# Normalising all chunks at the beginning of two causal stages, four score banks for their first maxima, and a reordered start of linear attention

## The reference

```python
x = x + sublayer_i(layernorm(x))        # i = 0 .. 7
```

```python
# 2 and 4, for each chunk of 512 tokens
scores = einsum('bhqd,bhkd->bhqk', q, k) * 8 ** -0.5
attn = softmax(where(causal, scores, -inf))      # in 4: -10000 for -inf
x = x + (einsum('bhqk,bhkd->bhqd', attn, v)) @ w_o + b_o
# 0: S_t = diag(exp(g_t)) S_{t-1} + k_t v_t^T ; o_t = q_t^T S_t, then a gate and a product
# 5: h = silu(x @ w1 * s1) * (x @ w2 * s2), two more layers, x @ w3 * s3
```

## Time and profile before

| what | value |
|---|---|
| three runs | 1694.02, 1687.55, 1692.11 us; median 1692.11 us |
| profiled execution | 1689.31 us, span 1687.6 us |
| TensorE's clock over the span | 0.883 of the full clock granted |
| busy share of the span | TensorE 83%, VectorE 62%, GpSimd 45%, ScalarE 44% |
| stage 0 | begins with VectorE at 8.44 us |
| stage 2 | from 321.7 us |
| stage 4 | from 642.4 us |

### The profile page before, as it was taken

How to read it: one execution, slowest core, us unless ns; L and a number is a source line. 1 busy time by engine, 2 the same in 40 slices (tenths; PEclk the granted TensorE clock), 3 DMA queues, 4 the chain that set the end, 5 groups by cost and what they waited for, 6 DMA issues and landing times. The chain is left out here.

```text
span 1687.6 us, 24930 instructions
## 1 busy us (share of the span) xinstructions
PE 1395.5 (83%) x8907; PEld 849.4 (50%) x8907; DVE 1042.6 (62%) x2864; ACT 747.3 (44%) x1169; POOL 763.4 (45%) x833
## 2 busy tenths in 40 slices
PE   5576688789998795999977999899999999985193
PEld 3354566644454562444435777555554545534062
DVE  5766678567884646688833222578778777757112
ACT  4554244336665341566644333455455454430041
POOL 5442344423432555354443442356555455563533
PEclk9688789859999796699978999799999999997597
DMA  3000004200000322000001020000000000003213
GB/s 97 7 8 1 34 22 193 85 1 1 1 2 1 129 63 97 1 2 1 2 0 53 1 100 1 1 1 1 1 1 1 1 1 1 1 1 125 63 51 100
DMA packets 29562, 52.74 MB, mean 31 GB/s; under 512 B 3216, under 2 KB 24592, under 8 KB 27264
## 3 DMA queue, kind: packets, MB, share of 16 engines
q1 hardware_dynamic: 26144, 44.36, 7.5%
q0 software_dynamic: 3296, 6.78, 1.2%
HBM read 29.07 MB, written 21.02 MB: 30 GB/s over the span
## 5 line engine op out<-in xcount | busy, mean ns | idle before, releaser
L2502 DVE CUSTOM_DVE_ANT_0 s_masked_scores<-s_for_max,s_mask_qk 128x128 bf16<-128x128 f32 (+3 forms) x512 | 227.0, 486 | 58.3 <-PE s_for_max L2323 56.4
L2863 POOL TENSOR_TENSOR wbuf<-s_probs 128x1024 f32<-128x1024 f32 x64 | 152.0, 2374 | 201.9 <-ACT s_probs L3022 201.9
L3022 ACT ACTIVATE s_probs<-s_scores 128x1024 f32<-128x1024 f32 x128 | 132.2, 1033 | 202.2 <-PE s_scores L2944 202.2
L2270 POOL TENSOR_SCALAR_AFFINE_SELECT s_probs<-s_probs 128x256 f32<-128x256 f32 x256 | 99.9, 407 | 247.7 <-ACT s_probs L2429 149.6
L3064 DVE TENSOR_REDUCE s_negmax<-s_for_max 128x2 f32<-128x1024 f32 x126 | 152.2, 1208 | 21.4 <-PE s_for_max L2919 21.3
L2323 PE MATMUL s_for_max<-s_k_stack,s_q_stack 32*128 32x128 f32 (+3 forms) x512 | 142.6, 441 | 26.9 <-DVE s_max_wide L2502 17.5
L3071 DVE RECIPROCAL s_recip<-s_pv_and_sums 128x128 f32<-128x128 f32 x128 | 116.6, 934 | 47.3 <-PE s_pv_and_sums L2970 47.3
L2323 PEld LDWEIGHTS s_for_max<-s_k_stack,s_q_stack 32*128 32x128 f32 x512 | 72.3, 205 | 128.8 <-DVE s_max_wide L2502 87.0
L2429 ACT ACTIVATE s_probs<-s_scores 128x1024 f32<-128x1024 f32 x128 | 127.4, 1024 | 14.0 <-PE s_scores L2344 13.7
L2957 PE MATMUL s_pv_and_sums<-s_probs,s_v 128*64 128x512 f32 x512 | 123.9, 605 | 0.9 <-DVE wbuf L3079 0.9
L2358 PE MATMUL s_pv<-s_probs,s_v_and_one 128*32 128x512 f32 (+3 forms) x1024 | 96.9, 474 | 1.5 <-DVE s_o L2521 1.5
(11 more groups left out here) (574 smaller groups left out, 3431.3 us busy)
## 6 DMA issues: line engine op xcount, KB each, us to landing
rows_by_expert<-s_empty_rows SPq DMA_DIRECT2D x8, 1032.0 KB, 10.5
s_w<-extra SPq DMA_DIRECT2D x2, 2048.0 KB, 10.1
wbuf<-w SPq DMA_DIRECT2D x1, 3460.0 KB, 11.2
s_generators<-extra SPq DMA_DIRECT2D x1, 2898.0 KB, 12.8
wbuf<-w SPq DMA_DIRECT2D x1, 2888.0 KB, 9.7
wbuf<-w SPq DMA_DIRECT2D x1, 2124.0 KB, 8.1
dispatched<-s_empty_slots SPq DMA_DIRECT2D x1, 2064.0 KB, 8.5
s_rows<-dispatched SPq DMA_DIRECT2D x8, 258.0 KB, 2.8
```

The costliest lines, as they stand in the source:

```text
L2270: last = nc.gpsimd.affine_select(out=diag, in_=diag, compare_op=ALU.is_ge, fill=0.0, base=0, pattern=[[0, diag.shape[1]], [1, P]], channel ...
L2502: last = nc.vector.tensor_tensor_reduce(out=junk[:, m % 2, at:at + n], in0=p1[m % 2][:, at:at + n], in1=mask[:, S - n:S], scale=1.0, scala ...
L2863: nc.gpsimd.tensor_tensor(added[half], probs[:, g % 2, 2 * half, :, :], probs[:, g % 2, 2 * half + 1, :, :], ALU.add).then_inc(s_added, 1)
L3022: nc.scalar.activation(probs[:, g % 2, j, :, :], p2[:, :, :], ACT.Exp, scale=dh ** -0.5).then_inc(s_exp, 1)
```

## The change

1. Start: each of the four transfers of x has a semaphore of its own; SyncE no longer waits for them, and VectorE waits for a chunk before its statistics.
2. Stage 0: TensorE makes 10, 2, 2 and 5 idle products (`spare_products`, of the bf16 identity into an unused bank) at the start and between its first steps, and waits for the weights only ahead of the first projection; the values of chunk 0 stand behind the sums of the log decay on TensorE, its gates behind factors 0 and 1 on ScalarE, and its copies behind the first scaled keys on VectorE.
3. Stages 2 and 4: the rows of all chunks are normalised, by VectorE, turned and copied in the beginning, into idle halves of p2, no longer through `pm`. The first 20 units of maxima take four banks in turn (p1 and p2[1]'s halves). The first exponentials wait for the turned rows and these units. GpSimd makes the low parts and adds the bias ahead of the first cut (stage 2: all chunks; stage 4: hs and bias of two chunks, the other two in single steps between cuts).
4. Stage 5: the rstd of chunk 1 stands behind one low part of the weights instead of five.
5. Stage 6: `ones` is cleared ahead of the rstd.

```diff
+    def spare_products(self, bank, n):
+        for _ in range(n):
+            self.nc.tensor.matmul(bank, self.identb[:, :],
+                                  self.identb[:, :].unsqueeze(1).broadcast_to([P, TPC, P]), start=True, stop=True)
...
# stage 0, TensorE
-            pe.wait_ge(sh.wsem[stage], 16)
+            unused = ps_a[:, heads - 1, :]
+            sh.spare_products(unused, 10)
+            pe.wait_ge(ln.s_rstd, 1)
+            sh.spare_products(unused, 2)
...
             ln.turned(pe, 0)
+            sh.spare_products(unused, 2)
+            pe.wait_ge(sh.wsem[stage], 16)
             project(0)
             ln.turned(pe, 1)
-            values(0)
+            sh.spare_products(unused, 5)
             pe.wait_ge(s_const, 5)
             sums(0)
             same(0)
+            values(0)
             project(1)
...
# stage 0, ScalarE
-            gates(0)
             sums(0)
             factors_all(0)
             factors(0, range(2))
+            gates(0)
             project(1)
             factors(0, range(2, 4))
...
# stage 0, VectorE
             log_decay(0)
-            values(0)
             for c in range(2, B):
                 ln.scaled(dve, c)
             near_first(0)
             scaled(0, range(2))
+            values(0)
             gate_input(1)
...
# stage 5, GpSimd
-            split.gpsimd(pool, range(1, 2 + n))
+            split.gpsimd(pool, range(1, 2))
+            ln.rstd_of(pool, 1)
+            split.gpsimd(pool, range(2, 2 + n))
...
# stages 2 and 4, the plan
-    for c in range(1, B):
-        behind(("max", QUADS * c - 2, 3), ("ln", c))
+    plan.insert(plan.index(("q", 0)), ("rows", 1))
+    behind(("q", 0), ("ln", 1))
+    behind(("q_stack", 0), ("rows", 2), ("rows", 3))
+    behind(("k", 0), ("ln", 2))
+    behind(("max", 0, 1), ("ln", 3))
...
+    turned_in = [None, p2[0][:, 0:S], p2[0][:, S:2 * S], p2[0][:, 0:S]]
+    ring = [p1[0], p1[1], p2[1][:, 0:S], p2[1][:, S:2 * S]]
...
+    def unit_bank(m):
+        return ring[m % 4] if m < EARLY_UNITS else p1[m % 2]
...
+    def bank_last_read(m):
+        if m < EARLY_UNITS:
+            return m - 3
+        return m - 3 if m < EARLY_UNITS + 2 else m - 1
...
# GpSimd
-        ln.rstd_of(pool, 0)
+        for c in range(2):
+            ln.rstd_of(pool, c)
+        pool.wait_ge(ln.s_xn, TPC)
         nc.gpsimd.memset(mask[:, :], 0.0).then_inc(s_mask, 1)
...
-        ln.rstd_of(pool, 1)
+        for c in range(2, B):
+            ln.rstd_of(pool, c)
+        pool.wait_ge(s_stack, 2)
...
-        ln.scaled_by(nc.gpsimd, pool, 1)
-        add_bias(0)
-        for c in range(2, B):
-            ln.rstd_of(pool, c)
+        for c in range(1, B):
+            ln.low_part_by(nc.gpsimd, pool, c)
+        if s_hs is None:
+            for c in range(B):
+                add_bias(c)
+        else:
+            for c in range(2):
+                for step in range(1 + TPC):
+                    make_hs(pool, c, step)
+                add_bias(c)
...
-            c = q // QUADS + 1
-            if c < B and q % QUADS == 0:
-                ln.low_part_by(nc.gpsimd, pool, c)
-            if c + 1 < B and q % QUADS == 1:
-                ln.scaled_by(nc.gpsimd, pool, c + 1)
-            if c < B and q % QUADS == 2:
-                add_bias(c)
+                c, step = divmod(q - 1, 2 + TPC)
+                if s_hs is not None and r == 0 and 0 <= c < B - 2:
+                    if step <= TPC:
+                        make_hs(pool, c + 2, step)
+                    else:
+                        add_bias(c + 2)
...
# TensorE
+            elif n == 0:
+                pe.wait_ge(ln.ready, B)
+            else:
+                pe.wait_ge(s_neg, EARLY_UNITS)
...
             elif item[0] == "ln":
-                odd_bank(item)
-                ln.turned(pe, item[1], pm)
+                if item[1] == 3:
+                    pe.wait_ge(ln.ready, 2)
+                ln.turned(pe, item[1], turned_in[item[1]])
...
# VectorE
+        ln.stats_of(dve, 1)
         ln.scaled(dve, 0)
         dve.wait_ge(sh.wsem[stage], 16)
         set_bias()
         st.end()
+        ln.stats_of(dve, 2)
         before_vector(dve)
-        ln.stats_of(dve, 1)
         ln.low_part(dve, 0)
-        for c in range(2, B):
-            ln.stats_of(dve, c)
-        dve.wait_ge(s_mask, 2)
-        dve.wait_ge(s_wide, 1)
+        ln.stats_of(dve, 3)
...
+            if item[0] == "rows":
+                ln.scaled(dve, item[1])
...
+                if m == 0:
+                    dve.wait_ge(s_mask, 2)
+                    dve.wait_ge(s_wide, 1)
```

More of the change, by code:

```diff
@@ L1978, in _ @@
                     nc.gpsimd.tensor_copy(empty[:, :, D], empty_i[:, :]).then_inc(s_empty, 1)
-                if c + 1 < B:
+                if c and c + 1 < B:
                     ln.rstd_of(pool, c + 1)
@@ L2214, in causal_attention @@
     plan = causal_plan()
-    odd = [item for item in plan if item[0] in ("q", "k", "maxT", "v", "oT", "y", "ln")]
+    odd = [item for item in plan if item[0] in ("q", "k", "maxT", "v", "oT", "y")]
+    turned_in = [None, p2[0][:, 0:S], p2[0][:, S:2 * S], p2[0][:, 0:S]]
[6 more added lines that the diff above has]
+        return m - 3 if m < EARLY_UNITS + 2 else m - 1
     block = ctx.enter_context(nc.Block())
@@ L2222, in emptied @@
             return s_stack, 2 * n + "qk".index(what) + 1
-        return {"maxT": s_sub, "v": s_v32, "oT": s_oTs, "y": s_x, "ln": ln.ready}[what], n + 1
+        return {"maxT": s_sub, "v": s_v32, "oT": s_oTs, "y": s_x}[what], n + 1
     @block.sync
@@ L2318, in scores_for_max @@
                 pe.wait_ge(s_stack, 2 * q + 2)
-            if m >= 2:
-                pe.wait_ge(s_neg, m - 1)
+            if bank_last_read(m) > 0:
+                pe.wait_ge(s_neg, bank_last_read(m))
             for x, i, at in max_units(u):
                 rows, n = slice(32 * x, 32 * x + 32), (i + 1) * P
-                last = nc.tensor.matmul(p1[m % 2][:, at:at + n], stacks[0][rows, q % SLOTS, i * P:n],
+                last = nc.tensor.matmul(unit_bank(m)[:, at:at + n], stacks[0][rows, q % SLOTS, i * P:n],
                                         stacks[1][rows, q % SLOTS, 0:n], start=True, stop=True)
@@ L2420, in _ @@
             elif item[0] == "ln":
-                ln.copied(act, item[1], pm[:, :])
+                ln.copied(act, item[1], turned_in[item[1]])
             elif item[0] == "exp_done":
@@ L2611, in first_rows_scalar, with make_hs @@
             ln.copied(act, 0)
[L2613 removed]
+        def make_hs(pool, c, step):
             ts = slice(c * TPC, (c + 1) * TPC)
[L2615 to L2620 removed]
+            if step == 0:
+                pool.wait_ge(ln.s_mv, (c + 1) * TPC)
+                nc.gpsimd.tensor_scalar(rstd[:, ts], ln.mv[:, ts, 1], LN_EPS, 1.0, ALU.add, ALU.mult).then_inc(s_once, 1)
+                pool.wait_ge(s_once, 2 * c + 1)
+                nc.gpsimd.tensor_tensor(rstd[:, ts], rstd[:, ts], sh.mhalf[:, ts], ALU.pow).then_inc(s_once, 1)
+            else:
+                t = c * TPC + step - 1
+                pool.wait_ge(s_once, 2 * c + 2)
                 nc.gpsimd.tensor_scalar(sh.hs[:, t, :], sh.x[:, t, :], ln.mv[:, t, 0:1], rstd[:, t:t + 1],
                                         ALU.subtract, ALU.mult).then_inc(s_hs, 1)
[L2623 removed]
         ca, cab = gen["ca_w"], gen["ca_b"]
```

44 lines of the change are left out of this document (18 added, 26 removed).

## The result

The kernel after takes 1668.3 us (median of four runs, 1662.25 to 1669.23) against 1691.5 before: ratio 0.9866, 95% interval 0.9843 to 0.9890, faster by more than half a per cent. On another chip, in the same series as the last experiments, the ratio was 0.9886 (0.9860 to 0.9912). The prediction was 1663.1, in a range of 1648 to 1676.

| stage | before | after | difference | predicted |
|---|---|---|---|---|
| start and stage 0, to stage 1's begin | 197.37 | 197.47 | +0.1 | -1.3 |
| 2 | 227.80 | 220.23 | -7.6 | -9.7 |
| 4, attention | 226.11 | 215.98 | -10.1 | -9.2 |
| 5 | 156.08 | 152.51 | -3.6 | -6.0 |
| all others | 880.2 | 879.8 | -0.4 | 0 |

What follows compares the result with a forecast made beforehand. One chain of eight stages on one core; in the causal beginnings no engine is saturated, two score banks making TensorE and VectorE wait in turn. 1.3 + 9.7 + 9.2 + 6.0 = 26.2 us off 1689.3 gives 1663.1, range 1648 to 1676.

Steps and rivals of the forecast that it cites:

- Stage 0: Start and stage 0: earlier x shrinks against one added table load and possible standstill; -1.3 us, bounds gain 5, loss 1.
- Stages 2 and 4, banks: Beginnings of stages 2 and 4: four banks remove VectorE's waits for maxima, 2.6 to 5.2 us; -4.0 each.
- near 0: Sign: VectorE's waits for maxima in the first 20 units would be near 0.
- The shift: Stage 2's begin: statistics of chunks 1 and 2 moved into waits; -0.9 us (0 to -1.05); in stage 4 -0.4.
- The first change of chunk: Stages 2 and 4: TensorE's 0.74 and VectorE's 3.17 us standstills as bounds; -1.8 us each stage.
- The second and third: Later chunk changes in stages 2 and 4, at full clock: 12.49 to 11.00 us, 1.49 each; -3.0 a stage.
- rival C: Stages 2 and 4: without turned rows at the chunk change the clock rises late; slower, 1690 and more; chance 0.05.
- GpSimd in stage 4: Ahead of stage 4's first cut: 6.1 us of work added to 14.15 idle, cut 4.4 earlier; 3 to 4 slack left.
- Stage 5: Early rstd brings scaling before h is needed: gap goes, 3.0 us; clock stays up, another 3.0; -6.0 (-3 to -6.5).
- A: Rival: denser beginnings raise the clock early, about 6 us a stage; 1657 for one stage, 1651 both; chance 0.27.
- B: Rival: the beginning gives little, TensorE held by projections and transposes, stage 5's clock falls; about 1675; 0.18 with D.
- D: Rival: banks do nothing, the exponentials' wait on 20 units replacing removed waits; 1671; counted with B, together 0.18.

Runs made afterwards that it cites:

- old order: Kernel after with chunk 0's values and gates back in their old places in stage 0, single waits and idle products kept; 1663.2 us in one run.
- two banks: Kernel after with the first 20 units of maxima on two banks in turn and first exponentials not waiting for them; 1678.9 us, in another series.
- kernel before with idle products: Kernel before plus only idle products in the causal stages' beginnings and quads 0 to 3; first reciprocals 67.8 and 63.2 us, stage 5 152.7.
- after twice: Two profiles of the kernel after, the second unchanged on the combined kernels' chip; stage 5 152.5 and 152.4 us.
- idle products: Kernel after plus idle products in TensorE's waits of both causal stages' beginnings; stage 2 215.0 us, stage 4 215.7.
- x at once: Kernel with stage 0's old order and idle products, SyncE again waiting for all of x before stage 0; stage 1 begins at 194.3 us.
- filled changes: Kernel after with one score product of the fourth unit made five times in quads 2, 6 and 10; stage 2 218.8 us, stage 4 220.2.
- idle in quads: Kernel after plus idle products in causal stages' beginnings and three ahead of each q and k projection of quads 1 to 3; stages 210.3 and 210.5 us.
- no idle: Kernel with stage 0's old order, without the nineteen idle products and their wait; stage 1 begins at 197.1 us.
- scaling first: Kernel after with stage 5's chunk 1 normalised on VectorE before the first h, GpSimd waiting for it; stage 5 151.3 us.
- combined kernel: Kernel after with stage 0's old order, stage 5's scaling first and idle products in beginnings and first quads; 1655.2 us, ratio to before 0.9764.

## Why the prediction was right, and where it was not

The total was right to 5 us. Stages 2 and 4 gave about what was forecast, in the main for the reasons given; stage 5 gave 3.6 of 6.0 us, and not for the reason given; and stage 0 came out within 1.4 us of its forecast only because two large errors cancelled, which is luck.

*Stage 0 (-1.3, measured 0).* Two steps failed. "The nineteen idle products cost nothing ... a higher clock from them would help projections that wait for weights anyway": they did cost nothing (the first projection begins at 10.25 with them and at 10.14 without), but the projections behind the weights ran at half speed before, and the idle products are worth 7.5 us of the stage with the old order. And the price of the moved values and gates, put at one table load and up to one standstill (1.28 and 3.6), is 7.9 us: what was missed is what is queued behind them, chunk 1's projections on TensorE (8.8 us later), their copies on ScalarE and then the factors. The table load itself was priced well: the gate starts at 29.68, 1.29 us after the load does, so the drain that the Trainium skill adds ("ScalarE: Activation LUTs", "What ACT_TABLE_LOAD costs") doesn't show in this case.

*Stages 2 and 4, banks (-4.0 each).* Right: 3.7 us at the first exponential in both, by the kernel with two banks, and by the cause that was named, VectorE's waits: 7.0 to 3.7 up to the table load. But the reading under it was short: the earlier trace rows stops ahead of a wait of 1.55 us, so the upper bound was 6.8 and not 5.2, and the sign "near 0" for these waits did not come; over half of them stayed. That TensorE's own load keeps them is plausible, but no run varies it.

*The shift (-0.9).* Right at about 1.0 in stage 2, in the execution where stage 2 begins with the clock low (table load at 33.52 behind the begin: 38.25 - 33.52 = 4.7, less the banks' 3.7). In the profiled execution another 1.4 came from the clock, still up for the first 1.5 us of the stage, in the products of the low-rank weights. This was in none of the terms. In stage 4 it gave 0.7 where 0.4 was said (34.25 to 29.77, less 3.7). That VectorE takes over the normalising cost nothing, as said: the two chunks fit into the wait ahead of k_stack(0), which went from 2.55 to 0.50.

*The first change of chunk (-1.8).* Right in stage 2, 2.3; in stage 4 it gave 2.7. *The second and third (-3.0).* Half right: the second fell from 12.50 to 10.99, and from 12.86 to 11.00 in stage 4, as the rows said. The third gave 0.07 and 0.45, because the clock fell in it. That steady quads can lose the clock was in none of my terms; rival C had it as a late rise only. Stage 2 then adds up: 8.4 up to the first reciprocal and 1.5 at the second change, less 1.5 for the fall in a plain quad and 0.9 behind the last reciprocal, is 7.6 with rounding. That it ends within 2.1 us of the -9.7 is partly luck: the clock gave 1.4 at the stage's begin, in no term either, and took 3.8 at the third change, in the plain quad and at the end.

*GpSimd in stage 4.* Slack mis-sized: 3 to 4 us forecast, none measured, as its work began only behind the first stacks, after a wait of 4.1 us. The cut came at most 0.1 us late, so the term stood.

*Stage 5 (-6.0, measured -3.6).* The step that failed is "the scaling comes before h is needed": beside three of GpSimd's products it takes 4.02 us, not 2.05, and the gap stayed. The other half, that the clock stays up, happened, but not for the gap's sake: it stayed up with a gap of 3.65 in the kernel before with idle products, and fell in three kernels with the change. In the seven kernels with either order of stage 5 where the first low stretch ended by 11.7 us behind the begin (before with idle, after twice, stage 0's old order, two banks, idle products, x at once), the stage took 152.4 to 152.7; in the four where it ended at 11.8 to 12.2 (before, filled changes, idle in quads, no idle), 155.9 to 156.1. So what part 4 of the change gives by itself is nothing that these runs show, 0.3 us at most in either group; its 3.6 us go with when the clock first rises. Where the clock rises late the gap does seem to matter: in the kernel with the scaling first, with no gap, it rose at 12.2 and the stage took 151.3; in the combined kernel, again without it, it rose at 11.5 and the stage took 151.3, too.

*Rivals.* A did not come: the clock rose 8 us earlier in each stage, with the work that was earlier (the first reciprocals by 8.4 and 7.2), not in the first quads. By its own sign, a low stretch that ends 65 and 61 us behind the begin, the forecast would have been wrong, with 56.1 and 53.7; but that sign left out that the forecast itself moves this work by 6 to 7 us. The kernels with idle products show that an early rise can be had. B and D fell with the banks' 3.7 us, C with a clock that rose earlier and not later.

What stays open: whether turned rows at the changes made falls rarer. With them, no fall between 60 and 160 us in four stages; without them and without filling, 15 in 22. Beyond 160 us there is one with them, too, in the kernel before with idle products. This points to the turned rows' work, and the filled kernel, with no fall in two more stages, points the same way, but it can't tell it from chance, and no run puts the turned rows alone back at the changes.

## What to carry to other kernels

An operation moved within one engine's queue is priced by what is queued behind it, on every engine that this holds up, and not by its own duration: here moved values and gates that were priced at 1.3 us of table load and up to 3.6 of standstill cost 7.9. Before a stage of a chain of dense products, idle products in an unused bank can be worth more than the reordering of real work, where the first real products stand on the path: here 7.5 us in stage 0. And a gain that rests on the clock staying up is to be seen in several executions, or by the neighbouring stages' shift, before it is credited to an edit.

## What the runs showed of the hardware that was not expected

With the same instructions stage 5 takes 152.5 or 156.0 us, and which of the two goes with a few tenths of a microsecond in when the clock first rises behind its begin (11.7 and less, or 11.8 and more). A quad of the causal stages takes 10.4 or 11.9, by whether the clock falls in it. VectorE's normalising of a 128x128 tile takes 0.34 us alone and 1.30 to 1.32 beside GpSimd's products of 128x512, each of three tiles in a row, while these take 1.50, 1.26 and 1.26 us where one alone takes 1.28: VectorE bears nearly all of it. In the kernel without idle products the window from 10 to 18 us has this row:

```profile
10.00:18.00 8.00, 7.86 (x15) 3.36 (x16) 5.08 (x23) 1.17 (x2) 0.52 (x2) 1.00 0.20 84
```

The granted clock reads 1.00, while the products in it take nearly twice as long (1.88 us) as the same ones at 29.57 (1.02), so ahead of its first change that column is better checked against durations. And stage 3, which no edit touches, took 92.8 and 92.9 us in the first two traces and 97.1 to 100.8 in all later ones, which is why whole times are compared only within one series.
